# Three units of attention with unread products in front of the maxima's products

## The chip, the cores and the metric

The program runs on one core of one Trainium2 chip. The metric is the device time of one execution in microseconds (us). Three runs of the kernel before gave 2369.28, 2373.66 and 2376.51 us, a median of 2373.66.

## The reference

Nine stages follow one another on 2048 tokens of 128 channels. Three of them hold a causal softmax attention with 16 heads of 8 channels, one in the first layer and two in the later `_L1_ffn` calls:

```python
scores = jnp.einsum('bqhd,bkhd->bhqk', q, k) / jnp.sqrt(jnp.float32(D))
causal = jnp.tril(jnp.ones((T, T), dtype=bool))
scores = jnp.where(causal, scores, jnp.float32(-1e+30))
p = jax.nn.softmax(scores, axis=-1)
y = jnp.einsum('bhqk,bkhd->bqhd', p, v).reshape(B, T, C)
```

The first layer's attention normalizes q and k differently; its scores, softmax and sums have the same form.

## The kernel before

`attention_stage` is called three times, once for each of these layers. It works on 16 units: four groups of four heads, each with four blocks of 512 queries (`UNITS`, pairs of group and block). In the first group the blocks come in the order 0, 1, 2, 3, so unit 0 has one block of 512 keys, unit 1 two, unit 2 three and unit 3 four.

Every unit needs two things. First the row maxima: for each of four tiles of 128 queries, each key block c and each of four heads, PE computes one product of queries and keys (`max_product`, L1176) into one of three PSUM banks, `stat` (`ring`, `RBANKS = 3`), and DVE reduces it to one column (L1295) or, in the unit's own block, masks and reduces it (L1292). These are 16, 32 and 48 products in units 0, 1 and 2. Heads 0 and 2 lie in rows 0 to 63 of the operands and heads 1 and 3 in rows 64 to 127, so a product uses 64 rows of PE's array, and two neighbours (h even, h odd) can stream at the same time: a pair. Each product waits until DVE has read the product three before it (`stat_used`).

Then the steps, one for each tile of 128 keys: `scores` (L1224, two pairs of products into `score`), the exponentials on ACT (L1125, into `probs`), POOL's causal cut (L1083) and `pv` (L1238, which uses all 128 rows and four narrow strips of columns). Between maxima and steps stands the shift: when a unit's maxima are all found, POOL cuts them into two parts, PE turns them (L1204), ACT copies them, and a DMA writes them into two spare rows of the queries, so that the scores come out with the maximum subtracted. The unit's first scores wait for that DMA. At the end PE turns the unit's sums (L1211).

The order on PE is fixed in the program. `attention_plan` deals the products of the maxima out to thirds of the steps (`FILL`); PE then runs scores, a few products, pv, a few products, scores, a few products, and so on, in order. Units 0 and 1 have little or nothing of earlier units beside them, since the pipeline is only being filled.

The operand of the keys, `uk`, has all 128 rows loaded before a unit's first product (`fill` waits for `begun` or `loaded`, and for the padding rows).

Of the kernel before, what the change touches and what calls it, by code (L numbers as in the profile page):

```python
# [22 lines left out]
P = 128  # L23
NT = T // P
D = C // H
BANK = 512
# [9 lines left out]
NG = H // HG  # L36
PAIRS = HG // 2
GBUFS = 2
M0, INNER = 64, 16
E, DFF = 4, 512  # L40
SLOTS = NT + E - 1
# [58 lines left out]
def rounded(ap):  # L100

    return ap.bitcast(F32R)

def head_rows(h):

    return slice(HROWS * (h % 2), HROWS * (h % 2) + HROWS)
# [33 lines left out]
def parts_stored(k):  # L141

    return [k.counter(f"parts_stored{c}") for c in range(NQ)]
# [794 lines left out]
def attention_plan():  # L938
# [9 lines left out]
    ends = [last[(g + 1) * NQ - 1] for g in range(NG)]  # L948
    free = [ends[g - GBUFS] + LOAD_STEPS if g >= GBUFS else -1 for g, _ in UNITS]
    weight = [1.0] * len(steps)  # L950
# [28 lines left out]
def attention_stage(k, w, v, parts_dram, first_rows, last_parts, scale, y, first_norm=None):  # L979
# [3 lines left out]
    nc = k.nc  # L983
    STEPS, FIRST, LAST, STREAM, FILL, SLOT, SHIFTS, OUTS = attention_plan()
    NU, NS = len(UNITS), len(STEPS)
    RBANKS, PSLOTS = 3, 6
    counts = []
    with ExitStack() as ctx:
        uq, uk = [first_rows[0], first_rows[2]], [first_rows[1], k.sb("group_k", [P, PAIRS, T], F32, ctx)]
# [10 lines left out]
        ring = [k.ps(f"stat{n}", [P, BANK], ctx) for n in range(RBANKS)]  # L1000
        sc = [k.ps(f"score{n}", [P, 2, BANK], ctx) for n in range(2)]
        acc = k.ps("pv", [P, BANK], ctx)

        loaded, begun = [k.counter(f"group_loaded{b}") for b in range(GBUFS)], [k.counter(f"block{c}_rows_loaded") for c in range(2)]
        cleared = [k.counter(f"shift_rows_cleared{b}") for b in range(GBUFS)]
        stored = parts_stored(k)
        padded = [k.counter(f"rows_padded{b}") for b in range(GBUFS)]
        shift_in = [k.counter(f"shift_rows_loaded{n}") for n in range(2)]
# [16 lines left out]
        def loads_of(g):  # L1025
            return NL * (g // GBUFS + 1)

# [3 lines left out]
        def load_shift_rows(eng, u, heads):  # L1031
            g, j = UNITS[u]
            for h in heads:
                at = HROWS * (h % 2) + KROWS
                rows = uq[g % GBUFS][at:at + SHIFT, h // 2, j * BANK:(j + 1) * BANK].rearrange("n (i q) -> n i q", q=P)
                eng.dma_start(rows, mxt[h * SHIFT * QC:(h + 1) * SHIFT * QC, u % 2, :]).then_inc(shift_in[u % 2].sem, 16)

        with nc.Block() as block:
# [128 lines left out]
            def _(pe):  # L1167
                def max_product(n):

                    u, s, c, h = STREAM[n]  # L1170
                    g, j = UNITS[u]
                    b, at, rows = g % GBUFS, j * BANK + s * P, head_rows(h)
                    width = (s + 1) * P if c == j else BANK
                    if n >= RBANKS:
                        pe.wait_ge(stat_used.sem, stat_used.at(n + 1 - RBANKS))
                    nc.tensor.matmul(ring[n % RBANKS][:, 0:width], rounded(uq[b][rows, h // 2, at:at + P]), rounded(uk[b][rows, h // 2, c * BANK:c * BANK + width]),  # L1176
                                     start=True, stop=True, tile_position=(rows.start, 0)).then_inc(stat_full.sem, 1)

                def fill(t, third):
                    for n in FILL.get((t, third), []):  # L1180
                        u, s, c, h = STREAM[n]
                        g = UNITS[u][0]
                        if (s, c, h) == (0, 0, 0):
                            if u < 2:
                                pe.wait_ge(begun[u].sem, begun[u].at(NL))
                            else:
                                pe.wait_ge(loaded[g % GBUFS].sem, loaded[g % GBUFS].at(loads_of(g)))
                            if u == 0:
                                pe.wait_ge(padded[0].sem, padded[0].at(NPADS * 16))
                            if g >= GBUFS:  # L1190
                                pe.wait_ge(cleared[g % GBUFS].sem, cleared[g % GBUFS].at(2 * 16 * (g // GBUFS)))
                            elif g == 1:
                                pe.wait_ge(padded[1].sem, padded[1].at(NPADS * 16))
                        max_product(n)
# [1479 lines left out]
```

## Time and profile before

| | |
|---|---|
| median of three runs | 2373.66 us |
| the profiled execution, its own time | 2371.53 us |
| span of its instructions | 2369.8 us |
| around the span | 1.7 us |
| PE busy | 1926.9 us (81%) |
| DVE busy | 1669.7 us (70%) |
| ACT busy | 1374.1 us (58%) |
| mean granted clock of PE | 0.883 |

A busy PE is one with a product anywhere between start and modelled end; products overlap, so this is not PE at its peak. The stretches of units are read from DVE's rows: a unit's maxima end where DVE reduces them to `row_max` (L1269). In the first attention stage that is at 72.9, 94.3 and 132.3 us for units 0, 1 and 2.

### The profile page before, as it was taken

Reading aid. Unit: us, or ns where it says so; the run is one execution under the profiler, and the core shown is the slowest. Engines: PE = TensorE matmul, PEld = TensorE weight load, DVE = VectorE, ACT = ScalarE, POOL = GpSimd, SP = SyncE. Lnnn points to the kernel's source line nnn. Section 1 sums busy time; section 2 is a strip of 40 time slices with the busy share of each in tenths; the row PEclk is TensorE's granted clock in tenths of the full one; section 3 lists DMA queues with packets and bytes.
Section 4 is the critical chain, followed back from the end, with each engine's and each line's share of the span. In section 5 each row is a group of like instructions: output and inputs, shape, how many; then the busy total and the mean of one; then the engine's idle time right before and its main releaser. Section 6 shows DMA issues by size and latency. Waiting matters only on the chain. (4 is left out here: it accounts for less than half of the span.)

```text
span 2369.8 us, 38818 instructions
## 1 busy us (share of the span) xinstructions
PE 1926.9 (81%) x12970; PEld 1039.0 (44%) x12970; DVE 1669.7 (70%) x4197; ACT 1374.1 (58%) x2027; POOL 462.9 (20%) x816
## 2 busy tenths in 40 slices
PE   4899899975699974687899899957647999999839
PEld 3433333333477753464333333337334333333338
DVE  6798898747366777467798898632697887888423
ACT  4257767865388865435366677832544466677712
POOL 4110120110355430220101110133001010211233
PEclk9599999996899986897699999978866799999959
DMA  7242030001201000006132030014114411300034
GB/s 228 74 72 36 5 38 2 2 23 42 89 29 40 38 18 1 1 1 178 23 51 38 3 38 2 2 47 170 33 44 134 72 16 25 37 3 2 2 105 162
DMA packets 47527, 113.89 MB, mean 48 GB/s; under 512 B 11952, under 2 KB 21426, under 8 KB 43144
## 3 DMA queue, kind: packets, MB, share of 16 engines
q1 hardware_dynamic: 40308, 96.84, 17.4%
q0 software_dynamic: 5088, 11.24, 1.5%
q10 hardware_dynamic: 1964, 3.70, 0.4%
q8 instruction: 90, 1.47, 0.3%
q14 instruction: 77, 0.63, 0.1%
HBM read 62.39 MB, written 32.64 MB: 40 GB/s over the span
## 5 line engine op out<-in xcount | busy, mean ns | idle before, releaser
L1125 ACT ACTIVATE probs<-score 128x1024 f32<-128x1024 f32 x960 | 822.8, 897 | 428.1 <-PE score L1224 422.3
L1295 DVE TENSOR_REDUCE max_part<-stat 128x1 f32<-128x512 f32 x1152 | 724.4, 682 | 95.3 <-PE stat L1176 87.5
L1238 PE MATMUL pv<-probs,v_ones 128*9 128x512 f32 (+3 forms) x3840 | 457.7, 550 | 0.6 <-ACT out_turned L1118 0.6
L1292 DVE CUSTOM_DVE_ANT_0 masked_scores<-stat,mask_row 128x128 f32<-128x128 f32 (+3 forms) x768 | 346.9, 487 | 145.7 <-PE stat L1176 142.4
L1176 PE MATMUL stat<-first_group_k,first_group_q 64*128 64x512 f32 (+2 forms) x960 | 364.0, 493 | 36.3 <-DVE max_part L1295 13.0
L1176 PE MATMUL stat<-group_k,group_q 64*128 64x512 f32 (+2 forms) x960 | 337.6, 407 | 16.1 <-DVE max_part L1295 7.6
L1176 PEld LDWEIGHTS stat<-first_group_k,first_group_q 64*128 64x128 f32 x960 | 175.9, 214 | 283.4 <-DVE max_part L1295 174.3
L1176 PEld LDWEIGHTS stat<-group_k,group_q 64*128 64x128 f32 x960 | 157.9, 185 | 279.1 <-DVE max_part L1295 161.1
L1224 PE MATMUL score<-first_group_q,first_group_k 64*128 64x512 f32 x960 | 250.2, 421 | 32.0 <-ACT probs L1125 19.6
L1224 PE MATMUL score<-group_q,group_k 64*128 64x512 f32 x960 | 230.1, 418 | 40.5 <-ACT probs L1125 31.2
L1083 POOL TENSOR_SCALAR_AFFINE_SELECT probs<-probs 128x256 f32<-128x256 f32 x384 | 150.1, 408 | 235.7 <-ACT probs L1125 234.3
L1940 ACT ACTIVATE abs_act_ps<-abs_act_ps 128x1024 f32<-128x1024 f32 (+3 forms) x176 | 167.5, 952 | 43.4 <-PE abs_act_ps L1895 39.8
L1224 PEld LDWEIGHTS score<-first_group_q,first_group_k 64*128 64x128 f32 x960 | 131.2, 198 | 53.7 <-ACT probs L1125 29.6
L1224 PEld LDWEIGHTS score<-group_q,group_k 64*128 64x128 f32 x960 | 112.9, 186 | 89.5 <-ACT probs L1125 84.5
L1972 DVE TENSOR_REDUCE abs_part<-abs_dve_ps 128x512 f32 (+5 forms) x224 | 108.9, 515 | 60.7 <-PE abs_dve_ps L1909 60.6
L1895 PE MATMUL abs_act_ps<-head_k,head_q 128*128 128x512 f32 x352 | 117.8, 420 | 1.4 <-ACT abs_act_ps L1940 0.2
L1092 POOL CAST row_max_parts<-row_max 128x16 fp32r<-128x16 f32 x48 | 9.5, 198 | 559.6 <-DVE row_max L1269 559.6
L1238 PEld LDWEIGHTS pv<-probs,v_ones 128*9 128x9 f32 x3840 | 57.4, 88 | 120.3 <-issue 89.6
L2444 DVE TENSOR_TENSOR hidden<-value_ps,gate 128x512 f32<-128x512 f32 x38 | 26.3, 691 | 116.8 <-PE value_ps L2348 116.8
L1100 POOL TENSOR_TENSOR qkv<-out_rows,inv_denominator 128x128 f32<-128x128 f32 x48 | 19.6, 408 | 373.1 <-DVE inv_denominator L1276 373.1
L1849 POOL TENSOR_SCALAR own_positive<-own_scores 128x2048 f32<-128x2048 f32 x16 | 85.8, 5362 | 0.0
L1909 PE MATMUL abs_dve_ps<-head_k,head_q 128*128 128x512 f32 (+2 forms) x224 | 71.9, 346 | 0.0
(375 smaller groups left out, 2476.0 us busy)
## 6 DMA issues: line engine op xcount, KB each, us to landing
tile_wv<-expert_wv SPq DMA_DIRECT2D x38, 512.0 KB, 3.3
q_parts<-early_parts_t SPq DMA_DIRECT2D x14, 512.0 KB, 3.8
group_k<-k_parts SPq DMA_DIRECT2D x24, 256.0 KB, 11.9
group_q<-q_parts SPq DMA_DIRECT2D x24, 256.0 KB, 18.4
k_parts<-early_parts_t SPq DMA_DIRECT2D x8, 512.0 KB, 4.5
head_q<-q_parts SPq DMA_DIRECT2D x32, 128.0 KB
head_k<-k_parts SPq DMA_DIRECT2D x32, 128.0 KB
first_group_q<-pad_rows SPq DMA_DIRECT2D x6, 512.0 KB, 5.5
```

The source lines that it names most:

```text
L1083: nc.gpsimd.affine_select(tile, tile, [[0, 2], [1, P]], ALU.is_ge, 0.0, base=0, channel_multiplier=-1).then_inc(cut.sem, 1)
L1125: nc.scalar.activation(probs[:, n % PSLOTS, :, 0:width], sc[m % 2][:, :, 0:width], ACT.Exp, scale=scale).then_inc(slot_read.sem, 1)
L1176: nc.tensor.matmul(ring[n % RBANKS][:, 0:width], rounded(uq[b][rows, h // 2, at:at + P]), rounded(uk[b][rows, h // 2, c * BANK:c * BANK + ...
L1224: last = nc.tensor.matmul(sc[m % 2][:, i, 0:BANK - f], rounded(uk[b][rows, hp, kt * P:(kt + 1) * P]), rounded(uq[b][rows, hp, j * BANK + f ...
L1238: last = nc.tensor.matmul(acc[32 * h:32 * h + D + 1, f:BANK], v9[:, kt, g * HG + h, :], probs[:, (2 * t + h // 2) % PSLOTS, h % 2, 0:BANK ...
L1292: nc.vector.tensor_tensor_reduce(masked[:, at % 2, 0:width], ring[n % RBANKS][:, 0:width], w["mask_row"][:, BANK - width:BANK], 1.0, NEG, ...
L1295: nc.vector.reduce_max(into, ring[n % RBANKS][:], AX.X).then_inc(stat_used.sem, 1)
L1849: nc.gpsimd.tensor_scalar(sa[:, par, :], sm[:, par, :], 0.0, None, ALU.max).then_inc(abs_ready.sem, 1)
L1895: ins = nc.tensor.matmul(a_ps[slot][:, b:min(b + BANK, width)], rounded(qm[:, par, i * P:(i + 1) * P]), rounded(km[:, par, at + b:at + min ...
L1909: ins = nc.tensor.matmul(out[:, 0:width], rounded(qm[:, par, i * P:(i + 1) * P]), rounded(km[:, par, at:at + width]), start=True, stop=True)
L1940: nc.scalar.activation(ps, ps, ACT.Abs, accum_out=part[:, bass.ds(h, 1), i, 0:1]).then_inc(a_used.sem, 1)
L1972: nc.vector.tensor_reduce(part[:, bass.ds(h, 1), i, slot:slot + 1], d_ps[n % DRING][:, 0:width], AX.X, ALU.add, apply_absolute_value=True) ...
```

## The change

A table `UNREAD = (2, 1, 1)` gives the number of extra products for units 0, 1 and 2. In front of each even head's product, after its wait for the bank, PE computes so many products of the keys with themselves: 128 rows, 128 columns of weights, 512 columns streamed, into the bank that the pair's first product overwrites next. Nobody reads them and they signal nothing.

```diff
+UNREAD = (2, 1, 1)
...
                     if n >= RBANKS:
                         pe.wait_ge(stat_used.sem, stat_used.at(n + 1 - RBANKS))
+                    if u < len(UNREAD) and h % 2 == 0:
+                        for _ in range(UNREAD[u]):
+                            keys = rounded(uk[b][:, h // 2, c * BANK:(c + 1) * BANK])
+                            nc.tensor.matmul(ring[n % RBANKS][:], keys[:, 0:P], keys, start=True, stop=True)
                     nc.tensor.matmul(ring[n % RBANKS][:, 0:width], rounded(uq[b][rows, h // 2, at:at + P]), rounded(uk[b][rows, h // 2, c * BANK:c * BANK + width]),
                                      start=True, stop=True, tile_position=(rows.start, 0)).then_inc(stat_full.sem, 1)
```

That is 16 extra products in each of units 0 and 1 and 24 in unit 2, 56 in a stage and 168 in the program. Nothing else moves; in the changed kernel the maxima's products are on L1181, the extra ones on L1180, and the scores on L1229.

On PE, the start of unit 0 in the first attention stage before (`stat` and `score` are PSUM tiles, the number is the buffer's; the last figures are rows of the result by columns streamed):

```order
L1176 MATMUL stat_84<-first_group_k,first_group_q 128x128
L1176 MATMUL stat_85<-first_group_k,first_group_q 128x128
L1176 MATMUL stat_86<-first_group_k,first_group_q 128x128
L1176 MATMUL stat_84<-first_group_k,first_group_q 128x128
L1176 MATMUL stat_85<-first_group_k,first_group_q 128x256
L1176 MATMUL stat_86<-first_group_k,first_group_q 128x256
```

The same place on PE now:

```order
L1180 MATMUL stat_84<-first_group_k 128x512 x2
L1181 MATMUL stat_84<-first_group_k,first_group_q 128x128
L1181 MATMUL stat_85<-first_group_k,first_group_q 128x128
L1180 MATMUL stat_86<-first_group_k 128x512 x2
L1181 MATMUL stat_86<-first_group_k,first_group_q 128x128
L1181 MATMUL stat_84<-first_group_k,first_group_q 128x128
L1180 MATMUL stat_85<-first_group_k 128x512 x2
L1181 MATMUL stat_85<-first_group_k,first_group_q 128x256
L1181 MATMUL stat_86<-first_group_k,first_group_q 128x256
```

Between any two pairs two whole products have come in; a narrow pair of 128 columns now follows 1024 columns that nobody reads.

On PE in unit 2 of the same stage, from the turn of unit 1's maxima (`row_max_parts`) through the first scores that wait for the shift's DMA, before:

```order
L1204 MATMUL score_88<-ident,row_max_parts 32x128
L1224 MATMUL score_87<-first_group_q,first_group_k 128x512 x2
L1176 MATMUL stat_86<-first_group_k,first_group_q 128x128
L1176 MATMUL stat_84<-first_group_k,first_group_q 128x128
L1176 MATMUL stat_85<-first_group_k,first_group_q 128x128
```

The same place on PE now, up to the next pv:

```order
L1209 MATMUL score_88<-ident,row_max_parts 32x128
L1229 MATMUL score_87<-first_group_q,first_group_k 128x512 x2
L1180 MATMUL stat_86<-first_group_k 128x512
L1181 MATMUL stat_86<-first_group_k,first_group_q 128x128
L1181 MATMUL stat_84<-first_group_k,first_group_q 128x128
L1180 MATMUL stat_85<-first_group_k 128x512
L1181 MATMUL stat_85<-first_group_k,first_group_q 128x128
L1243 MATMUL pv<-probs,v_ones 9x256 x4
```

Behind the scores that waited, an extra product now stands in front of the first product that DVE waits for, and scores, pairs and pv are each separated by one.

## Rows read from the trace of the kernel before

**Rows 1.** The page: the span, and PE's granted clock in 40 slices.
```profile
span 2369.8 us, 38818 instructions
...
PEclk9599999996899986897699999978866799999959
```

**Rows 2.** Windows, first stage: units 0 to 2, then 9 and 10; PE, PEld, DVE, ACT, POOL busy, clock.
```profile
65.20:72.90 7.70, 7.21 (x18) 4.47 (x18) 7.53 (x33) 1.90 (x1) 1.85 (x1) 0.50 0.80 274
73.00:94.40 21.40, 17.95 (x57) 9.35 (x56) 17.00 (x50) 6.63 (x9) 2.04 (x6) 0.58 0.35 51
94.40:132.40 38.00, 32.79 (x130) 14.34 (x133) 26.81 (x66) 12.68 (x15) 1.91 (x6) 0.60 0.00 1
...
285.80:305.80 20.00, 18.14 (x137) 7.51 (x133) 17.16 (x50) 14.14 (x20) 3.49 (x10) 1.00 0.01 2
305.90:335.00 29.10, 26.96 (x209) 12.06 (x201) 27.09 (x68) 18.01 (x30) 10.50 (x28) 1.00 0.45 57
```

**Rows 3.** Windows of the third stage: units 2 and 3, columns as in rows 2.
```profile
1820.50:1859.00 38.50, 33.54 (x125) 14.68 (x125) 26.88 (x65) 12.88 (x15) 1.91 (x6) 0.55 0.00 1
1859.00:1900.20 41.20, 38.81 (x218) 15.62 (x221) 36.94 (x84) 22.68 (x27) 4.21 (x12) 0.92 0.66 103
```

**Rows 4.** Idle before L1176 (us, times) in 65 to 132.4: what ended it.
```profile
  DVE max_part L1295: 17.6, 33
  DVE max_part L1292: 7.3, 23
```

**Rows 5.** The same for units 9 and 10, 285.8 to 335.
```profile
  DVE max_part L1295: 12.8, 25
  DVE max_part L1292: 6.7, 14
```

**Rows 6.** Windows of 3.4 us, first stage, columns as in rows 2.
```profile
66.50:69.90 3.40, 3.40 (x10) 2.27 (x9) 3.31 (x17) 1.90 (x1) 0.55 (x1) 0.50 1.08 378
...
87.00:90.40 3.40, 3.40 (x14) 1.00 (x14) 1.81 (x6) 0.00 (x0) 0.00 (x0) 0.50 0.00 0
90.40:93.80 3.40, 2.56 (x12) 1.07 (x8) 3.26 (x9) 0.98 (x2) 0.00 (x0) 1.00 0.00 0
```

**Rows 7.** Windows, PE alone, where retention's 128-row products begin: length, busy, clock.
```profile
653.60:657.00 3.40, 3.40 (x15) 0.50 0.01 2
657.00:660.40 3.40, 3.40 (x13) 0.50 0.00 0
660.40:663.80 3.40, 3.27 (x15) 1.00 0.00 0
```

**Rows 8.** Timeline (start, length): pair, turned sums over 128 rows, pair, at half clock.
```profile
123.98 0.28 PEld L1176 LDWEIGHTS stat<-first_group_k,first_group_q 64*128 64x128 f32 x1 [0.32 <-DVE max_part L1295]
124.70 0.71 PEld L1211 LDWEIGHTS score<-ident,out_turned 128*128 128x128 f32 x4 [0.44 <-issue]
...
125.75 0.28 PEld L1224 LDWEIGHTS score<-first_group_q,first_group_k 64*128 64x128 f32 x2 [0.33 <-issue]
...
126.34 0.63 PE L1176 MATMUL stat<-first_group_k,first_group_q 64*128 64x512 f32 x2
```

**Rows 9.** Timeline: the same sequence at full clock.
```profile
152.47 0.18 PEld L1176 LDWEIGHTS stat<-first_group_k,first_group_q 64*128 64x128 f32 x1 [0.75 <-DVE max_part L1295]
...
152.90 0.42 PEld L1211 LDWEIGHTS score<-ident,out_turned 128*128 128x128 f32 x4 [0.24 <-issue]
...
153.49 0.19 PEld L1224 LDWEIGHTS score<-first_group_q,first_group_k 64*128 64x128 f32 x2 [0.17 <-issue]
...
153.83 0.39 PE L1176 MATMUL stat<-first_group_k,first_group_q 64*128 64x512 f32 x2
```

**Rows 10.** Timeline: 128-row products of 512 columns at half clock.
```profile
659.04 1.05 PE L1895 MATMUL abs_act_ps<-head_k,head_q 128*128 128x512 f32 x2
659.89 0.82 PE L1909 MATMUL abs_dve_ps<-head_k,head_q 128*128 128x384 f32 x2
```

**Rows 11.** Timeline: unit 1's first scores, first stage.
```profile
103.89 0.80 PE L1224 MATMUL score<-first_group_q,first_group_k 64*128 64x512 f32 x2 [4.16 <-DMA first_group_q<-row_max_turned]
```

**Rows 12.** Timeline: unit 1's first maxima, second stage, with DVE's idle time before.
```profile
1114.16 2.48 DVE L1295 TENSOR_REDUCE max_part<-stat 128x1 f32<-128x512 f32 x4 [1.58 <-PE stat L1176]
```

## The prediction

> **What bounds the kernel now.** I read the page first: the span is 2369.8 us and PE's clock is below full in several of the 40 slices, among them the second and third, where the first attention stage begins [rows 1]. Then the windows of its units. Units 0, 1 and 2 take 7.7, 21.4 and 38.0 us at clocks of 0.50, 0.58 and 0.60, while units 9 and 10, with the same numbers of products as 1 and 2, take 20.0 and 29.1 us at 1.00 [rows 2]. The third stage repeats it: 38.5 us at 0.55 for unit 2, and even unit 3 loses something to the clock, 41.2 us at 0.92 [rows 3]. So three times per execution some 10 us lie in the slow clock's reach, and no more: DVE is busy for 26.8 of unit 2's 38.0 us [rows 2], and 4.2 us of the rest is PE waiting for the shift's DMA [rows 11], which no clock shortens. At the half clock PE isn't full either: products of the maxima found PE idle for DVE's release of a bank for 17.6 + 7.3 = 24.9 us between 65 and 132 us [rows 4]. That idle time is what can hide new work.
>
> **What the change adds.** Per stage 16 + 16 + 24 = 56 products of 128 rows by 512 columns; nothing is removed, no wait and no transfer added. What waits behind one is the pair's first product on PE, and DVE for that.
>
> The price of one has two parts. Streaming: two such products of retention start at 659.04 and the next at 659.89, so 0.43 us each at the half clock [rows 10], and half of that, 0.21, at full. The second part is the change between a product over 64 rows and one over 128. The trace has it where a unit's sums are turned. At the half clock a pair's weight load starts at 123.98 and the first 128-row weight load at 124.70: 0.72 us, of which 0.43 is the pair's stream, so 0.29 is lost. On the way back, the 64-row load starts at 125.75 and the third product in that row at 126.34: 0.59 less a stream of 0.43 is 0.16; ahead of it the loader stood idle for 0.33, in part while the last turn still streamed, so another 0 to 0.33; I take 0.19. Lost per round trip: 0.29 + 0.16 + 0.19 = 0.64 us, with ends 0.45 and 0.78 [rows 8]. At full clock the same reading gives 0.22 + 0.13 + 0.10 = 0.45 [rows 9]. So one extra product costs PE 0.43 + 0.64 = 1.07 us at half and 0.21 + 0.45 = 0.66 at full, and two in a row cost 0.85 + 0.64 = 1.49 at half.
>
> At the half clock this adds 8 × 1.49 = 11.9 us to unit 0, 16 × 1.07 = 17.1 to unit 1 and 24 × 1.07 = 25.7 to unit 2: 54.7 us per stage. The cover is PE's idle time of 24.9 us [rows 4]. Net 29.8 us later per stage. Unit 0 by itself checks this: its pairs stream 2 × (128 + 256 + 384 + 512) columns, 2.1 us, so PE needs 14.0 us against the 7.7 that the unit takes now [rows 2]. In stages 2 and 3 DVE waits about 1.6 us before unit 1 for rows that are being loaded [rows 12], and in the third stage about as long, which hides that much of unit 0's lateness: 28.2 each. All at half clock: 29.8 + 2 × 28.2 = 86 us. Below, the cost can be zero or negative if the clock rises; that is a rival.
>
> **Does the clock rise?** This decides. Busy is not enough: in 66.5 to 69.9 PE is busy for 3.40 of 3.40 us with 64-row products and stays at 0.50 [rows 6]. Nor are 128 rows enough: in 653.6 to 657.0 PE does nothing but 128-row products, busy throughout, and stays at 0.50 for that stretch and the next; only after the second, with wider products back to back, does it get 1.00 [rows 7, 10]. In unit 0 the extra products won't stream back to back: of every 1.6 to 1.9 us (1.49 plus the pair's 0.11 to 0.43) 0.64 goes into the two changes, in which the array stands. That looks more like the stretch that stayed at 0.50. In units 1 and 2, with one extra product per pair, the share lost is larger still, and PE, now the bound, loses its dense stretches around pv: the clock now rises after one of these (87.0 to 90.4), and falls again after 3.4 us [rows 6].
>
> So I expect half clock in units 0 and 1 and in the first half of unit 2, and a rise somewhere in unit 2, when pv and the turned sums come close together; once up it should stay, since PE then has steps and extra products to do. The half of unit 2 behind the shift (some 20 products, 10 extra) then costs about nothing instead of about 8 us, since at full clock 10 × 0.66 us lie beside 24.7 ÷ 2 us of DVE's work and PE's idle time there is of that size: 12.8 + 6.7 = 19.5 us in the 49.1 of units 9 and 10 [rows 5]. Per stage 29.8 − 8 = 21.8, and 28.2 − 8 = 20.2 in the other two: 62 us. Against the profiled execution, 2371.5 (span 2369.8 and 1.7 around it), that is 2433.5. The median of the runs is 2.1 us above that execution, so I forecast **2436 us**.
>
> **The rivals.**
> *The clock rises in unit 0 and the change pays* (the other side). For it: the extra products use the whole array, and more columns of it are then streamed than by pairs alone. Price and gain: the first 5 us of unit 0 go at 1.6 us a pair, which costs 2 us (0.4 in stages 2 and 3, where the loads hide the rest); unit 1 falls from 21.4 to unit 9's 20.0, unit 2 from 38.0 to unit 10's 29.1 plus the shift's wait of 4.4. That is +2 − 1.4 − 4.5 = −3.9, then −5.5 twice, and unit 3 of the third stage gets 2.6 back: −17.5, or 2356 us. It decides from the point where the stretch in unit 0 counts as enough for the clock, and it must survive the shift's wait. Against it are rows 7 and 8.
>
> The Trainium skill, "TensorE: Matmul & The Clock Gate", section "Why this matters for your kernels", says that TensorE should be kept busy without a pause to reach the higher clock. By that rule this rival would win, since the extra products leave PE no pause in unit 0; by the rows, PE busy without a pause from 66.5 to 69.9 and from 653.6 to 657.0 stayed at half, so I don't let the rule decide.
>
> *The clock rises early, falls in the shift's wait and comes back late.* PE idles 4.2 us there whatever its clock [rows 11]. Then unit 0 costs 2, unit 1 gains 1.4, and unit 2 behind the shift costs 8: some +8.5 per stage, +25, 2399 us.
>
> *It never rises before unit 3*: the whole 86 us, 2460.
>
> *Nothing to see*: changes between 64 and 128 rows cost little here, idle time covers the products, the clock stays as it is: 2374. Against it, unit 0, where 6.8 us of streaming alone (16 × 0.43) come to a unit of 7.7 us in which DVE already waits for nothing. That the extra products are dropped can be left out: they stand in PE's order.
>
> **How the numbers follow.** Forecast 0.50 (2415 to 2450), never rising 0.12, rises and falls 0.15, early rise 0.15, nothing to see 0.08. A measurement of this kernel can tell about 0.3%, 7 us, from no change: faster is below 2366.5, slower above 2380.8. Slower: 0.50 + 0.12 + 0.14 and a little of the last = 0.77; the same 0.09; faster 0.14, nearly all of the early rise. The range that holds 8 in 10 leaves out the early rise and half of no change: 2380 to 2468.
>
> **What would show it.** In the profile after, unit 0 of the first stage should end near 79 instead of 72.9, at 0.50 throughout; L1180 should have rows of two every 1.6 to 1.9 us, with 0.6 us of them in changes; DVE should wait for PE in units 0 and 1; unit 2 should be 8 to 18 us longer. A clock of 1.00 before unit 0's end, or units 1 and 2 shorter than now, would prove the forecast wrong; a round trip well below 0.45 us would show that the price was.

## The result and the profile after

The changed kernel takes 2466.8 us (median of four runs, 2460.47 to 2473.98) against 2373.28 us for the kernel before on the same chip: a ratio of 1.0405, 95% interval 1.0376 to 1.0434. The forecast of 2436 us had the sign, the bound and the price of an extra product right; the rise of the clock that it counted on in unit 2 did not come, and the loss is 93.5 us where 62.3 were forecast. The result came nearest to the rival "never rises before unit 3" (2460).

The profiled execution took 2473.98 us. Its page, the span, the engines' busy time, and PE's granted clock in 40 slices, answers to [rows 1]:

```profile
span 2471.1 us, 39147 instructions
...
PE 2038.2 (82%) x13131; PEld 1075.9 (44%) x13138; DVE 1677.8 (68%) x4197; ACT 1374.0 (56%) x2027; POOL 462.1 (19%) x816
...
PEclk8559999995889996897599999977866599999959
```

PE has 111.3 us more of busy time, DVE only 8.1. Of the two slices with the first attention stage, the second and the third, only the second was at 5 before; now both are, and the tenth and the twentieth went from 6 to 5.

Next the windows, which answer to [rows 2, 3] (length; then busy time of PE, PEld, DVE, ACT, POOL; clock; DMA share and GB/s). First units 0, 1, 2 and 3 of the first stage, then unit 2 of the third in two pieces:

```profile
69.10:82.60 13.50, 13.50 (x33) 6.21 (x31) 7.15 (x31) 1.91 (x1) 0.37 (x1) 0.50 0.42 142
82.80:110.70 27.90, 26.40 (x73) 11.42 (x71) 17.47 (x48) 6.63 (x9) 2.03 (x6) 0.50 0.24 39
110.90:167.00 56.10, 51.90 (x150) 19.82 (x148) 28.31 (x64) 12.77 (x15) 1.90 (x6) 0.50 0.00 1
167.20:208.70 41.50, 39.27 (x214) 15.61 (x213) 36.81 (x84) 22.46 (x27) 4.20 (x12) 0.90 0.64 102
...
1910.50:1916.40 5.90, 4.43 (x20) 1.75 (x20) 5.08 (x9) 0.64 (x2) 1.90 (x6) 1.00 0.00 0
1916.40:1964.20 47.80, 45.08 (x128) 17.36 (x128) 23.16 (x56) 12.21 (x13) 0.00 (x0) 0.50 0.00 1
```

PE is busy for all 13.50 us of unit 0 and for 51.90 of unit 2's 56.10, and in the first stage the clock stands at 0.50 through all three units, 98 us in a row. In the third it comes out of unit 1 at 1.00, and in unit 2 it is lost after 5.9 us and stays at 0.50 for the other 47.8; the second stage goes the same way. It is lost in the shift's wait, in which PE has nothing to do. PE's timeline there (the clock falls at 1916.3):

```profile
1914.64 0.29 PE L1209 MATMUL score<-ident,row_max_parts 128*32 128x128 f32 x1
1919.08 0.80 PE L1229 MATMUL score<-first_group_q,first_group_k 64*128 64x512 f32 x2 [4.15 <-DMA first_group_q<-row_max_turned]
```

From the end of this wait to the end of unit 2 it takes 45.2, 45.2 and 45.1 us in the three stages, at 0.50 throughout, where it took 28.4, 28.9 and 29.2 before. The first stage's stretch, before and now:

```profile
103.90:132.30 28.40, 27.59 (x112) 12.47 (x116) 21.75 (x57) 12.04 (x13) 0.00 (x0) 0.64 0.00 1
...
122.10:167.30 45.20, 45.16 (x128) 17.33 (x128) 23.21 (x57) 12.21 (x13) 0.00 (x0) 0.50 0.00 0
```

That is 49.0 us more in three stages, as much as the whole of unit 2 lost in them: in sum, unit 2's loss lies behind the wait.

DVE's work has hardly grown (28.31 us in unit 2 against 26.81); it waits. The waits stand in the groups of DVE's instructions for 69 to 167 us (instructions, busy time and mean; idle time before them and what ended it):

```profile
L1300 DVE TENSOR_REDUCE max_part<-stat 128x1 f32<-128x512 f32 x48 | 31.3, 687 | 20.9 <-PE stat L1181 20.7
L1297 DVE CUSTOM_DVE_ANT_0 masked_scores<-stat,mask_row 128x128 f32<-128x128 f32 (+3 forms) x48 | 21.8, 488 | 24.7 <-PE stat L1181 24.7
```

The same two groups before, for 65 to 132.4 us:

```profile
L1295 DVE TENSOR_REDUCE max_part<-stat 128x1 f32<-128x512 f32 x48 | 30.0, 683 | 6.7 <-PE stat L1176 6.6
L1292 DVE CUSTOM_DVE_ANT_0 masked_scores<-stat,mask_row 128x128 f32<-128x128 f32 (+3 forms) x48 | 21.2, 487 | 9.0 <-PE stat L1176 8.7
```

DVE's waits for PE went from 6.6 + 8.7 = 15.3 us to 45.4 in one stage, 30.1 more, close to the 31.4 us by which units 0 to 2 of this stage grew. The waits for DVE on PE's side went the other way. What was 24.9 us before the maxima's products [rows 4] is now, in the lists of what ended the idle time before L1181 and, since the wait for the bank now stands in front of the extra products, before L1180, from 69 to 167 us (us, times):

```profile
  DVE max_part L1297: 1.5, 2
  DVE max_part L1300: 1.3, 1
...
  DVE max_part L1300: 4.6, 8
  DVE max_part L1297: 0.4, 1
```

So 17.1 of the 24.9 us are gone and 7.8 are left. These lists add up the idle time of the weight loader (PEld) and that of the products' stream (PE), and the loader can be idle while a product streams. For the stream alone, the rows of the maxima's products before (65 to 132.4 us) and now (69 to 167) are:

```profile
L1176 PE MATMUL stat<-first_group_k,first_group_q 64*128 64x512 f32 (+3 forms) x98 | 43.4, 632 | 4.8 <-DVE max_part L1295 1.8 <-PEq L709 1.2 <-DVE max_part L1292 0.5
...
L1181 PE MATMUL stat<-first_group_k,first_group_q 64*128 64x512 f32 (+3 forms) x98 | 41.0, 708 | 0.0
```

Only 2.3 us of the 24.9 were idle time of PE's stream; the rest is the loader's. PE now bounds the three units, but for the shift's wait.

Measured from unit 0's first reduction on DVE to unit 3's last, the three stages are 34.4, 28.7 and 25.1 us longer, 88.1 together. The extra products ahead of each stage's first pair delay it by 1.12 us more (67.64 to 68.76 below), 3.4 in three stages. That is 91.5, within 2 us of the difference of the medians. The profiled execution itself is 101.3 us longer in its span; the remaining 9.8 us lie in stages that the change doesn't touch (some 7.6 of them between the second stage's unit 3 and the third stage's unit 0), and two of the four runs were 13 us shorter than this one. I give these 9.8 us to nothing. In the profiles of all eleven kernels the time outside units 0 to 3 of the three stages lies between 2046.0 and 2064.7 us without following the change, so the units' lengths say more than a difference of a few us between single runs.

The price of an extra product can be read in the timeline of units 0 and 1 (start, length, count):

```profile
67.64 1.19 PE L1180 MATMUL stat<-first_group_k 128*128 128x512 f32 x2 [1.20 <-PEq L710]
68.76 0.47 PE L1181 MATMUL stat<-first_group_k,first_group_q 64*128 64x128 f32 x2
...
77.57 1.22 PE L1180 MATMUL stat<-first_group_k 128*128 128x512 f32 x2
78.72 0.79 PE L1181 MATMUL stat<-first_group_k,first_group_q 64*128 64x512 f32 x2
79.45 1.22 PE L1180 MATMUL stat<-first_group_k 128*128 128x512 f32 x2
...
87.63 0.79 PE L1180 MATMUL stat<-first_group_k 128*128 128x512 f32 x1
88.35 0.28 PEld L1181 LDWEIGHTS stat<-first_group_k,first_group_q 64*128 64x128 f32 x2 [0.44 <-issue]
89.07 0.79 PE L1180 MATMUL stat<-first_group_k 128*128 128x512 f32 x1
89.07 0.29 PEld L1180 LDWEIGHTS stat<-first_group_k 128*128 128x128 f32 x1 [0.44 <-issue]
```

With two extras: 77.57 to 79.45 is 1.88 us, less 0.85 for their stream and 0.43 for the pair's, leaves 0.60. With one: 87.63 to 89.07 is 1.44, less 0.43 and 0.43, leaves 0.58. The round trip between 64 and 128 rows costs 0.6 us at the half clock, where 0.64 was taken from [rows 8]. The loader's rows show what it consists of: at each change the loader stands idle for 0.44 us, as long as the product before streams, and then loads for 0.28 or 0.29 us; 0.44 + 0.28 are the 0.72 us from one change to the next (88.35 to 89.07). So each change adds the time of a load that could not go ahead, and two such loads are the 0.6 us. Between products of the same rows the load goes ahead, here with 64-row extra products at the half clock in experiment 9 below:

```profile
107.29 0.66 PE L1180 MATMUL stat<-first_group_k 64*128 64x512 f32 x2
107.29 0.36 PEld L1181 LDWEIGHTS stat<-first_group_k,first_group_q 64*128 64x128 f32 x2
107.72 0.34 PE L1181 MATMUL stat<-first_group_k,first_group_q 64*128 64x128 f32 x2
```

The product's weights are loaded while its extra product streams, and it starts 0.43 us after it: nothing is lost.

Where the clock comes back, in a window of the first stage's unit 3 (columns as above):

```profile
174.80:178.20 3.40, 3.05 (x22) 1.75 (x22) 2.72 (x7) 0.87 (x2) 0.77 (x2) 0.89 0.85 195
```

It rises at 175.5, 8 us into unit 3 and 10 us after the end of the last extra product (165.2); in the other two stages 5 us after it.

### The profile page after: what moved, and what is told of

The parts are those of the page before. It is cut to its first block and busy times, and to the rows that moved or that the text cites. A ratio compares the mean times of both kernels' runs of the same rounds, so it can differ in the third digit from the quotient of the medians.

```text
span 2471.1 us, 39147 instructions
## 1 busy us (share of the span) xinstructions
PE 2038.2 (82%) x13131; PEld 1075.9 (44%) x13138; DVE 1677.8 (68%) x4197; ACT 1374.0 (56%) x2027; POOL 462.1 (19%) x816
## 3 DMA queue, kind: packets, MB, share of 16 engines
q8 instruction: 91, 1.49, 0.3%
## 5 line engine op out<-in xcount | busy, mean ns | idle before, releaser
L1181 PE MATMUL stat<-first_group_k,first_group_q 64*128 64x512 f32 (+2 forms) x960 | 353.2, 507 | 16.7 <-DVE max_part L1300 9.9
L1181 PE MATMUL stat<-group_k,group_q 64*128 64x512 f32 (+2 forms) x960 | 337.4, 407 | 16.3 <-DVE max_part L1300 7.6
L1181 PEld LDWEIGHTS stat<-first_group_k,first_group_q 64*128 64x128 f32 x960 | 158.7, 215 | 281.7 <-DVE max_part L1300 132.0
L1181 PEld LDWEIGHTS stat<-group_k,group_q 64*128 64x128 f32 x960 | 157.8, 185 | 279.0 <-DVE max_part L1300 162.0
L1229 PE MATMUL score<-first_group_q,first_group_k 64*128 64x512 f32 x960 | 238.6, 423 | 32.1 <-ACT probs L1126 19.6
L1229 PE MATMUL score<-group_q,group_k 64*128 64x512 f32 x960 | 229.7, 417 | 40.7 <-ACT probs L1126 31.3
L1229 PEld LDWEIGHTS score<-group_q,group_k 64*128 64x128 f32 x960 | 112.6, 185 | 89.6 <-ACT probs L1126 84.6
L1229 PEld LDWEIGHTS score<-first_group_q,first_group_k 64*128 64x128 f32 x960 | 125.8, 201 | 52.2 <-ACT probs L1126 29.7
L1180 PE MATMUL stat<-first_group_k 128*128 128x512 f32 x168 | 120.3, 745 | 8.3 <-DMA first_group_q<-q_parts 6.0
L1101 POOL TENSOR_TENSOR qkv<-out_rows,inv_denominator 128x128 f32<-128x128 f32 x48 | 19.5, 407 | 376.3 <-DVE inv_denominator L1281 376.3
## 6 DMA issues: line engine op xcount, KB each, us to landing
head_q<-q_parts SPq DMA_DIRECT2D x32, 128.0 KB
head_k<-k_parts SPq DMA_DIRECT2D x32, 128.0 KB
```

What stands on the lines that cost most here:

```text
L1180: nc.tensor.matmul(ring[n % RBANKS][:], keys[:, 0:P], keys, start=True, stop=True)
L1229: last = nc.tensor.matmul(sc[m % 2][:, i, 0:BANK - f], rounded(uk[b][rows, hp, kt * P:(kt + 1) * P]), rounded(uq[b][rows, hp, j * BANK + f ...
```

## Experiments

All start from the changed kernel. A passage from 64-row to 128-row products and back is called a hand-over below. Theory A in all of them: PE's array stands still in a hand-over, this costs about 0.6 us a time, and it also keeps the clock at 0.50. The rivals are named in each expectation. The kernel before had medians of 2376.47 us (19 runs, 2364.70 to 2390.74) beside experiments 1, 2, 3 and 6, 2376.33 (17 runs) beside 4, 5, 7 and 8, and 2371.98 (13 runs, on another chip) beside 9. Unit lengths run from the unit's first to its last reduction on DVE; before they are 7.2, 21.2 and 37.8 us in the first stage (20.6 and 38.3, 38.4 for units 1 and 2 in the others), and 38.5, 38.5, 41.0 for unit 3.

**1. The same hand-overs with an eighth of the streaming.**

```diff
-                            nc.tensor.matmul(ring[n % RBANKS][:], keys[:, 0:P], keys, start=True, stop=True)
+                            nc.tensor.matmul(ring[n % RBANKS][:, 0:64], keys[:, 0:P], keys[:, 0:64], start=True, stop=True)
```

> The extra products stream 64 columns instead of 512; their number, rows and places stay as in the changed kernel. Theory A (the price is the change between 128 and 64 rows, about 0.64 us per round trip at the half clock, and it also keeps the array too idle for the full clock): each extra product still costs about 0.7 us, unit 0 of the first stage takes 8 to 9.5 us (13.5 in the changed kernel, 7.2 before), unit 2 about 45 to 48 (56.1 and 37.8), the clock stays at half, and the time is 2400 to 2420. Theory B (the price is the streamed columns, and the change of rows costs little): with 7 of 8 columns gone the three units are within 1 us of before, and the time is 2372 to 2380.

Measured: 2426.98 us, one run, 50.5 above the kernel before. Units 0, 1 and 2 take 9.5, 24.3 and 48.3 us in every stage. Unit 2 of the first stage:

```profile
100.70:149.00 48.30, 44.11 (x149) 20.34 (x148) 27.90 (x65) 12.85 (x15) 1.90 (x6) 0.50 0.00 1
```

54% of the loss stays when an eighth of the extra columns is streamed: most of this is the hand-overs, with the half clock that goes with them, and the clock is at 0.50 throughout units 0 to 2. The time is 7 us above theory A's range; unit 3, which lost 1.5, 2.9 and 4.0 us to the clock as well, is enough to account for that.

**2. No hand-overs: the same streaming in 64 rows.** Each of the pair's products gets its own 64-row extra product in the same half of the array.

```diff
-UNREAD = (2, 1, 1)
+UNREAD = (1, 1, 1)
-                    if u < len(UNREAD) and h % 2 == 0:
+                    if u < len(UNREAD):
-                            keys = rounded(uk[b][:, h // 2, c * BANK:(c + 1) * BANK])
-                            nc.tensor.matmul(ring[n % RBANKS][:], keys[:, 0:P], keys, start=True, stop=True)
+                            keys = rounded(uk[b][rows, h // 2, c * BANK:(c + 1) * BANK])
+                            nc.tensor.matmul(ring[n % RBANKS][:], keys[:, 0:P], keys, start=True, stop=True, tile_position=(rows.start, 0))
```

> One unread product of 512 columns in front of every product of units 0 to 2, over the same 64 rows as the product behind it, so that nothing changes between 64 and 128 rows; as many columns times rows as one 128-row product per pair. Theory A: the array streams without hand-overs, the clock rises within unit 0 and holds in unit 1, falls in the shift's wait and comes back within two or three stretches; units 0 to 2 take 60 to 65 us in the first stage (66.7 before, 98.1 in the changed kernel), and the time is 2355 to 2368. Theory B (unread columns cost PE time, and the clock does not answer to them): half clock stays, 80 us or more for the three units, 2400 to 2440.

Measured: 2390.76 us (10 runs), ratio 1.0049, interval 1.002 to 1.0077. Theory A's time was missed: it is 0.5% slower than before, not faster. The windows of units 0, 1 and 2 of the first stage say why:

```profile
67.90:76.80 8.90, 8.90 (x33) 7.18 (x32) 7.59 (x32) 1.91 (x1) 0.96 (x1) 0.50 0.69 235
77.00:102.20 25.20, 23.83 (x87) 16.20 (x87) 17.45 (x49) 6.63 (x9) 2.03 (x6) 0.50 0.30 44
102.50:139.70 37.20, 32.90 (x176) 17.06 (x179) 26.82 (x64) 12.77 (x15) 1.90 (x6) 0.85 0.00 1
```

In units 0 and 1 the clock did not rise, against my expectation (but for the last 4 us of the third stage's unit 1), and they pay 1.7 and 4 us. In unit 2, behind the shift's wait, it rose to full, and unit 2 is a little shorter than before; unit 3 is at 1.00 in all three stages. Without hand-overs 79 of the 93.5 us are gone (2390.76 is 14.3 above 2376.47), though 96 products over half the rows are streamed per stage instead of 56 over all rows.

**3. The same extra products in half as many places.** All of a pair of pairs' extras stand in front of head 0.

```diff
-                    if u < len(UNREAD) and h % 2 == 0:
-                        for _ in range(UNREAD[u]):
+                    if u < len(UNREAD) and h == 0:
+                        for _ in range(2 * UNREAD[u]):
```

> The same number of 128-row extra products, but all four (two in units 1 and 2) of two neighbouring pairs stand in front of the first, so half as many changes between 128 and 64 rows. Theory A: unit 0 takes 10.5 to 11.5 us instead of 13.5, the denser stream brings the full clock in units 0 or 1 at least in one stage, and the time is 2385 to 2430. Theory B: as in the changed kernel, 2455 to 2475, the clock at half in all three units.

Measured: 2454.47 us, one run. The time lies at the edge of theory B's range and well above theory A's. Unit 2 takes 47.6, 42.5 and 50.7 us at clocks of 0.61, 0.76 and 0.57 instead of 56.1, 53.7 and 53.7 at 0.50 and 0.55: fewer hand-overs, the same products, and behind the shift's wait the clock rises before the last extra product in the first two stages, though not in the third. But unit 1 takes as long as in the changed kernel (27.9, 27.1 and 27.5 us), and unit 0 takes 13.7 us, as there, where 10.5 to 11.5 were expected. PE's timeline of unit 0:

```profile
72.98 2.08 PE L1180 MATMUL stat<-first_group_k 128*128 128x512 f32 x4
74.98 1.01 PE L1181 MATMUL stat<-first_group_k,first_group_q 64*128 64x384 f32 x3
76.33 0.68 PE L1181 MATMUL stat<-first_group_k,first_group_q 64*128 64x384 f32 x1 [0.34 <-DVE max_part L1297]
```

After four extras in a row come three products, and the fourth must wait for DVE to free a bank; then DVE runs dry: it waits 8.5 us for PE in four such places. The ring of three banks can't carry DVE over the longer burst. My expectation had counted PE's time alone.

**4. More extra products in unit 0.**

```diff
-UNREAD = (2, 1, 1)
+UNREAD = (4, 1, 1)
```

> As the changed kernel, but four 128-row extra products per pair in unit 0 instead of two: more work, the same number of hand-overs. Theory A (the share of a pair's time that goes into hand-overs kept the clock down): in unit 0 the clock now rises to 1.00 within 10 us, unit 0 takes 13 to 16 us (13.5 in the changed kernel at half clock), unit 1 runs at or near full clock and takes 19.5 to 24 us (27.9), so that the kernel with more products is faster than the changed one up to unit 1's end, by 2 to 8 us per stage; 2440 to 2465. Theory B: 16 more products of 0.43 us per stage, unit 0 takes 20 to 21 us, the clock stays at half, 2485 to 2495.

Measured: 2466.51 us, one run, the same as the changed kernel with 48 more products of 128 rows, and just above theory A's range. Windows of 3.4 us from 74.7 on, in unit 0:

```profile
74.70:78.10 3.40, 3.40 (x12) 2.13 (x12) 1.25 (x5) 0.00 (x0) 0.00 (x0) 0.66 0.00 0
78.10:81.50 3.40, 3.40 (x15) 1.90 (x13) 2.45 (x11) 0.00 (x0) 0.00 (x0) 1.00 0.00 0
```

Before this rise PE ran four extra products and a pair every 2.5 us, 0.6 us of it in the hand-over; in the changed kernel it ran two and a pair every 1.55 to 1.88 us, also with 0.6 in the hand-over, and no rise came in unit 0. PE is busy for 3.40 of 3.40 us in both windows. Unit 0 lies in theory A's range; unit 1 does not: units 0 and 1 together take 41.1, 38.9 and 39.0 us where they took 41.4, 40.1 and 40.4, 0.3 to 1.4 us less in a stage where 2 to 8 were expected. Unit 2 is at 0.55 in all three stages (53.7 us each).

In the first stage the clock is at full from 77.0 to 87.2 and from 104.3 to 114.5. The first time it falls 3.7 us into unit 1, whose start has pauses on PE (0.89 us for POOL, 0.27 for DVE) beside its single extra products; which of the two brings it down is not shown. The second time it falls in the shift's wait, from 113.73 to 117.90:

```profile
117.90 0.80 PE L1229 MATMUL score<-first_group_q,first_group_k 64*128 64x512 f32 x2 [4.16 <-DMA first_group_q<-row_max_turned]
```

From 104.3 to the start of that wait it held at 1.00, with one extra product in front of each pair. Behind the wait it stays at 0.50 to the end of unit 2.

**5. Unit 2 alone.**

```diff
-UNREAD = (2, 1, 1)
+UNREAD = (0, 0, 1)
```

> The 128-row extra products of the changed kernel in unit 2 alone. Theory A: unit 2 costs what it does in the changed kernel, 52 to 57 us instead of 38, units 0 and 1 as before: 45 to 57 us more than before in all, 2420 to 2435. Theory C (the units' costs are not additive, since unit 2 recovers part of what units 0 and 1 lose): less than 40 us more.

Measured: 2434.26 us, one run, 57.9 above the kernel before. Unit 2 of the first stage:

```profile
95.30:151.50 56.20, 51.99 (x148) 19.79 (x148) 28.44 (x65) 12.87 (x15) 1.91 (x6) 0.50 0.00 1
```

It is 56.2 us long, at 0.50, with units 0 and 1 as they were before. Units 2 of the other stages take 56.0 and 55.9 us, also at 0.50. So unit 2's loss is its own and does not come from a clock that units 0 and 1 had kept down. The units' costs do not simply add up, though: units 0 to 3 lose 21.3, 20.3 and 22.7 us here by the profile, nearly all of it in units 2 and 3, which lost 53.5 us together in the changed kernel's three stages.

**6. 64-row extras, and the shift's wait filled.** As experiment 2, and 16 products of 128 rows that nobody reads between the turn of unit 1's maxima and unit 1's first scores, where PE has nothing to do for 4.2 us [rows 11].

```diff
+FILLER = 16
...
+                    if hp == 0 and u == 1 and t == FIRST[u]:
+                        keys = rounded(uk[b][:, 0, 0:BANK])
+                        for _ in range(FILLER):
+                            nc.tensor.matmul(sc[m % 2][:, 0, :], keys[:, 0:P], keys, start=True, stop=True)
```

> As the one with 64-row unread products, and 16 unread 128-row products into the score bank while PE waits for the shift of unit 1. Theory A: the clock no longer falls in that wait of 4.2 us, unit 2 runs at 1.00 and takes 33 to 35 us, and the time is 2 to 10 us below the run without the filling, 2348 to 2362. Theory B: the filling only delays the scores, 2 to 3 us per stage more than without.

Measured: 2372.03 us (10 runs), ratio 0.999, interval 0.9963 to 1.0017, no difference from the kernel before that can be told; theory A's time (2348 to 2362) was missed. Unit 2 takes 34.0, 36.5 and 36.5 us at 1.00, 0.88 and 0.89, which pays for most of what units 0 and 1 lose. Against experiment 2, which lacks the filler alone, it is 18.7 us less, and no run of the one lies within those of the other (2368.28 to 2377.35, 2380.53 to 2395.05). By the profiles units 0 to 3 account for 5.9 us of this; where the rest comes from is not shown.

**7. The two together, without the extras of units 0 and 1.** Experiment 6 with `UNREAD = (0, 0, 1)` and `FILLER = 11`.

> No extra products in units 0 and 1. While PE waits for unit 1's shift, 11 unread 128-row products back to back; in unit 2 one unread 64-row product in front of every product. Theory A (what counts for the clock is how densely the array streams; dense and without hand-overs it rises, in idle time this costs nothing): units 0 and 1 as before (7.2 and 21 us), full clock from the shift's wait on and through unit 2, which takes 33 to 35.5 us (38 before); 2360 to 2370 where the kernel before gives 2376. Theory B (unread products are only a load): unit 2 takes 40 us or more, 2380 to 2400.

Measured: 2363.88 us (12 runs, 2358.02 to 2371.78), ratio 0.9948, interval 0.9929 to 0.9968: 0.5% faster than the kernel before, a small gain but clear of no change. By the profiles units 0 to 3 are 8.2 us shorter in three stages, of 12.5 in the medians. Unit 2 in the first and second stage:

```profile
96.60:131.90 35.30, 33.48 (x187) 17.77 (x190) 26.67 (x65) 12.77 (x15) 1.90 (x6) 0.95 0.01 1
1134.50:1170.70 36.20, 36.05 (x187) 19.89 (x190) 26.78 (x65) 12.77 (x15) 1.90 (x6) 0.86 0.00 1
```

And the filled waits on PE's timeline:

```profile
102.15 2.80 PE L1229 MATMUL score<-first_group_k 128*128 128x512 f32 x11
106.45 0.51 PE L1234 MATMUL score<-first_group_q,first_group_k 64*128 64x512 f32 x2 [1.50 <-DMA first_group_q<-row_max_turned]
...
1140.74 4.56 PE L1229 MATMUL score<-first_group_k 128*128 128x512 f32 x11
```

The filler lies in a wait that is there anyway: in the first stage PE still waits 1.50 us for the DMA after it, in the second it fills it. Behind it the scores take 0.5 us where they took 0.80 [rows 11].

**8. The filler alone.** `UNREAD = (0, 0, 0)`, `FILLER = 11`.

> Only the 11 unread 128-row products in the shift's wait, no other extra product. Theory A: the clock rises after them, but unit 2 by itself does not hold it in its first microseconds in every stage, as before (1.00 for 3.4 us from 107.5, then 0.50); unit 2 takes 35 to 38 us, 0 to 8 us less than before in all. Theory B: unit 2 takes as long as before or longer by the last of the eleven, 38 to 40 us.

Measured: 2372.78 us, one run, not to be told from before. Unit 2 takes 37.3, 37.5 and 34.7 us at 0.68, 0.68 and 0.75. The rest of the first stage's unit 2 behind the filler:

```profile
105.20:112.00 6.80, 6.28 (x40) 3.03 (x39) 6.01 (x17) 3.73 (x5) 0.00 (x0) 1.00 0.00 0
112.00:132.60 20.60, 19.50 (x74) 7.70 (x78) 15.60 (x40) 8.48 (x9) 0.00 (x0) 0.67 0.00 1
```

The filler brings the clock to 1.00, and unit 2's own products do not keep it there.

**9. 64-row extras in unit 2 alone, no filler.** Experiment 2 with `UNREAD = (0, 0, 1)`.

> One 64-row extra product in front of each of unit 2's 48 products per stage, in the same half of the array as the product behind it; nothing in units 0 and 1, and none of the 11 products that filled the shift's wait before unit 1's first scores. Theory A (hand-overs between 64 and 128 rows are what cost; without them the extra streaming lifts the clock inside unit 2 and pays a little): unit 2 takes 35 to 37 us at a clock of 0.8 to 0.9 instead of 38, unit 3 takes 38.5 at 1.00 in all three stages, 2362 to 2372 us. Theory B (only the filled wait brought the gain of the version with both; the products in unit 2 alone are paid for): unit 2 38 us or longer, 2374 to 2385 us.

Measured: 2366.79 us (10 runs), ratio 0.9975, interval 0.9955 to 0.9995. Unit 2 takes 37.0, 37.1 and 38.0 us at 0.86, 0.86 and 0.78. The first stage's, whole and in pieces:

```profile
96.80:133.80 37.00, 32.56 (x175) 16.86 (x179) 26.78 (x65) 12.77 (x15) 1.91 (x6) 0.86 0.00 1
...
100.40:103.80 3.40, 2.02 (x8) 0.87 (x6) 2.97 (x5) 0.64 (x2) 0.41 (x1) 1.00 0.00 0
103.80:110.60 6.80, 3.87 (x22) 2.50 (x23) 0.91 (x7) 1.02 (x1) 0.00 (x0) 0.50 0.01 2
```

From the end of the shift's wait to the end of unit 2, here and in experiment 5:

```profile
106.70:133.80 27.10, 26.93 (x152) 14.52 (x156) 21.86 (x56) 12.13 (x13) 0.00 (x0) 0.93 0.00 1
...
106.40:151.50 45.10, 45.05 (x128) 17.33 (x128) 23.19 (x56) 12.23 (x13) 0.00 (x0) 0.50 0.00 0
```

Extra products in the same places as experiment 5's, as much of the array streamed through (twice the products, each over half the rows), and no hand-over for them: 37 us instead of 56, the clock at 0.86 instead of 0.50, and 63 us less in the whole (5.2 below its kernel before, where experiment 5 was 57.9 above). Behind the wait PE is busy almost all the time in both; the clock comes back at 110.6 here, 4 us behind it, and only at 159.9 there, behind the end of unit 2. This is the cleanest pair of the study. It changes the number of products along with their shape; that the shape alone matters rests on experiment 3 beside it. The pieces show what the filler is for: the clock rises ahead of the shift's wait, falls in it, stays down for 6.8 us, and comes back; in the first stage of experiment 7 it stayed up. There unit 2 is 1.7, 0.9 and 1.8 us shorter by the profiles. In the whole the two intervals overlap, so that the filler adds to the gain is not settled.

## Why the prediction was right or wrong

*What bounds: right. The cover: near in size, misread.* PE became the bound of units 0 to 2. But the 24.9 us of [rows 4] that I took for PE's idle time add up the loader's and the stream's; PE's stream was idle for DVE for only 2.3 us of them, and only for 1.5 us of the 19.5 of [rows 5]. With the measured price the 54.7 us of new work are 52.4, and 32.5 of them showed in the first stage (31.4 and 1.1 of delay), so some 20 us were absorbed. That this is near 24.9 is in part luck. The slack is better read as in the prediction's own check of unit 0: pairs that stream for 2.1 of 7.7 us leave room that a busy time of 7.21 us does not show.

*The price of an extra product: right.* 0.43 + 0.6 = 1.03 us against 1.07 at half clock, 1.45 against 1.49 for two. Experiment 1 shows the hand-over's part by itself. The Trainium skill, "TensorEngine Tiling (Array Packing)", section "Key Properties", says that a change of tiling mode drains TensorE; it gives no time, and the timeline agrees with it at 0.6 us per round trip.

*Units 0 and 1: right.* Unit 0 grew by 6.3 us; the forecast had it end at 79 instead of 72.9. It ended at 82.7, but the stage's first product began 2.4 us later (67.64 against 65.2), which is not the change's: in experiment 9, with nothing added to unit 0, its first reduction is at 68.1, and here, less the 1.1 us of the two extra products, at 68.2. From its first product unit 0 takes 7.4 us more, 1.1 above the forecast. The pairs came every 1.55 to 1.88 us where 1.6 to 1.9 were named. Unit 1 was at 0.50 in the first stage; in the other two it came up near its end, to a mean of 0.59 and 0.58, as it had before (0.58 and 0.57).

*All at the half clock, 86 us: right in size.* From unit 0's first reduction to unit 2's last it is 31.4, 26.1 and 26.1 us, 83.6, and 86.9 with the delay of the first pairs.

*The clock: the step that failed.* It was "a rise somewhere in unit 2", after which half of unit 2's extras would cost "about nothing instead of about 8 us". No such rise came: from the shift's wait to the end of unit 2 the clock stands at 0.50 for 45 us in every stage, and a clock of 1.00 that two stages brought from unit 1 was lost in that wait. So the 24 us that the rise was to save in three stages were paid. In the kernel before the clock came back for good at 128.0 in the first stage, 24 us behind the wait; now it came back at 175.5, 53 us behind it. I had argued that pv and the turned sums come close together in unit 2, but extra products stand among these groups too, and each brings its 0.6 us. I also took some 10 extra products to lie behind the shift, where the trace has 20 of the 24, and reckoned with 24.7 us of DVE's work, which stands in no row (26.81 in [rows 2]). The runs tie the missing rise to the hand-overs: the extras as 64-row products in the same place let the clock come back (experiment 9 against 5), half the hand-overs with the same products do so in two of three stages (experiment 3), and units 0 and 1 have no share in it (experiment 5). I had used this argument for units 0 and 1 and dropped it for unit 2 without a row that showed the difference.

*Unit 3: a term that was missing.* The sum ended with unit 2. Unit 3 lost 3.0 and 2.6 us in the first two stages, since the clock came back only 8 us into it; in the third it was late already before [rows 3], and unit 3 became 1.0 us shorter. That is 4.5 us net.

24 for the rise, 4.5 for unit 3 and 0.9 for the 86 that became 86.9 are 29.4 of the 31.2 us by which the measured loss (93.5) exceeds the forecast one (62.3).

*The rival of an early rise* had beside it the rule that TensorE should be kept busy (the Trainium skill, "TensorE: Matmul & The Clock Gate", section "Why this matters for your kernels"). Here PE is busy for all 13.50 us of unit 0 at 0.50; the measurement decides against the rule as far as busy time in the profile is meant. Experiment 4 shows that the rise does come with more 128-row products in a row, but their own time eats what it gives.

*The rival "rises early, falls in the shift's wait and comes back late"* had its second half right: wherever the clock stood at 1.00 when PE began that wait of 4.2 us, it fell before the wait ended, eleven times in the changed kernel and experiments 2, 3, 4 and 9. With unread products in the wait it stayed up (experiments 6 and 7, first stage).

What stays open: why the clock did not rise in units 0 and 1 of experiment 2, where 64-row products stream without hand-overs, though in experiment 6, with the same units 0 and 1, it rose at 90.9 in the first stage's unit 1. In its timeline the two halves of the array often take turns rather than overlap; that this is the reason was argued and not tried.

## What to carry to other kernels

Adding products to lift the clock paid here only where they need no change of the array's shape among the others (in the same rows as their neighbours) or lie in a wait that is there anyway, and then by 0.2 to 0.5% of the time; in units 0 and 1 it did not pay even so (experiment 2). Price a 128-row product among 64-row ones by its stream and the round trip, and read from the windows of the clock, not from PE's busy share, whether the stretch around it has a chance to rise. Before calling idle time cover, ask whose it is: the loader's or the stream's. If an argument keeps the clock down in one stretch, ask of the next stretch whether the same argument still holds before crediting a rise there.

## What the runs showed of the hardware

- A round trip between 64-row and 128-row products costs 0.6 us at the half clock whether one or two products stand between. It is two weight loads of 0.28 or 0.29 us, each of which begins only when the product before has streamed.
- Behind the shift's wait PE was busy for 45.05 of 45.10 us at a granted clock of 0.50 in experiment 5, and for 26.93 of 27.10 at a mean of 0.93 in experiment 9.
- A clock of 1.00 fell in the shift's wait of 4.2 us in all eleven cases in which it stood there when the wait began, at 1916.3, for example, in a wait from 1914.93 to 1919.08.
- 11 products of 128 rows and 512 columns in a row took 2.80 us in one stage and 4.56 in another, by the clock that they found.
